# State-space stage: ScalarE prepares the FP4 rounding term, with a new table of steps

## Chip, cores and metric

The kernel runs on one core of one Trainium2 chip. The metric is the device time of one execution in microseconds, as the median of several runs.

## What is computed

The whole is two transformer-like layers in float32. The change touches the first layer only: a Mamba block and an FP4 feed-forward block side by side on the same normalized input, for 8 sequences of 512 rows, 256 columns each. Cut to what matters:

```python
xn = layernorm(x)                                  # (8, 512, 256)
x  = x + mamba(xn) + fp4_ffn(xn, w_gate, w_up, w_down)

def mamba(x):                                      # d_inner 512, d_state 16
    x_in, z = split(x @ W_in.T)
    u = silu(causal_conv4(x_in) + conv_b)
    d_raw, B, C = split(u @ W_xproj.T)             # 16, 16, 16
    delta = softplus(d_raw @ W_dt.T + b_dt)
    h[t] = exp(delta[t] * A) * h[t-1] + (delta[t] * u[t]) * B[t]
    y[t] = sum_n(h[t] * C[t]) + D * u[t]
    return (y * silu(z)) @ W_out.T

def fp4_quant_dequant(x):                          # blocks of 16 along the last axis
    scale = maximum(max(abs(xb)) / 6, 1e-12)
    idx = searchsorted([.25, .75, 1.25, 1.75, 2.5, 3.5, 5.], abs(xb / scale))
    return grid[idx] * sign(xb) * scale            # grid 0 .5 1 1.5 2 3 4 6

def fp4_ffn(x, ...):                               # hidden width 704
    h = silu(q(x) @ q(w_gate).T) * (q(x) @ q(w_up).T)
    return q(h) @ q(w_down).T
```

## The kernel before

The program has an FP4 preparation of the weights, then the stage `mamba_and_fp4_ffn`, then the second layer's attention and local-attention stages, which the change does not touch. The stage works through 8 batches (sequences). Each batch has 32 steps, here called units 0 to 31: unit u is one scan over 512 time steps for 128 channels and two states. Four channel groups of 8 units each make a batch.

In unit u the engines do this:

- ScalarE (ACT, L829 and L831) fills one of two halves of the PSUM tile `ps_dA` with exp(delta * A), called a fill below. It may start when unit u-2's product has left that half; for units 0 and 1 it waits for the whole batch before.
- GpSimd (POOL, L581) multiplies B with delta * u into a ring `hb` of eight buffers.
- VectorE (DVE) scans (L670), does the unit's extra work, and multiplies by C (L681).
- TensorE (PE, L1053) sums the product into `ps_y` with an identity matrix. At units 8, 16, 24 and at unit 0 of the next batch VectorE takes that sum and gates it (`gate_y`, L632), so these units wait until TensorE has summed the group before.

Everything else is woven in between as extra work behind a unit's own work: the projections and convolutions of the next batch, the four row tiles of the hidden layer of this batch, and the output sums of the batch before. Each engine works strictly in the order written. Which unit carries which piece is a table of numbers at the head of the function: `GATE`, `SILU`, `UP`, `XIN`, `CONV`, `Z`, `TURN_H` and so on, one entry for each tile or channel group. The buffers and semaphores decide whether a piece is ready.

The FP4 rounding is `fp4_part`, in three parts in three different units. Part 0 makes the blocks' scales. Part 1 (L125 to L127) multiplies by the inverse scale, takes the exponent bits of the result with a bitwise AND into the tile `work`, and turns them into 1.5 * 2^22 times the power of two, not less than 1.5 * 2^22. Part 2 (L129, L130) adds `work` and subtracts it, which rounds. It runs once a batch for the next batch's input `xn` (128 x 1024, units 11, 15, 18) and four times for the hidden tiles `h` (128 x 704, units 5 to 7, 22 to 24, 25 to 27, 29 to 31). All of these run on VectorE, with a semaphore between one and the next. The batches before the first and after the last carry parts of the work only: a prologue prepares batch 0 with no scans beside it, and the last batch prepares no other.

Of the kernel before, what the change touches and what calls it, by code (L numbers as in the profile page):

```python
# [215 lines left out]
def mamba_and_fp4_ffn(nc, io, W, x1_dram, bc_dram, NB):  # L216
# [22 lines left out]
    TURN_H, TAKE_H = [(9, 10), (28, 28), (30, 30), (1, 0)], [(11, 12), (28, 28), (31, 31), (0, 6)]  # L239

    FFN_SUM, TAKE_SUM = 28, 29
    X1, TAKE_X1 = [0, 1, 3, 5], [2, 6]

    Z, TAKE_Z, MOVE_Z = [13, 16, 26, 22], [15, 17, 27, 22], 17
# [7 lines left out]
    XD, TAKE_XD = 18, 19
    STORE = 14

    DT, ABS, LN = [19, 20, 24, 5], [20, 21, 24, 6], [24, 22, 24, 8]
    SOFT = [("abs", 0), ("relu", 0), ("exp", 0), ("abs", 1), ("relu", 1), ("exp", 1), ("ln", 1), ("abs", 2), ("relu", 2),
            ("exp", 2), ("ln", 0), ("ln", 2), ("abs", 3), ("relu", 3), ("exp", 3), ("ln", 3)]


    NORM, SCALE_X, DU, ADD = [3, 4, 5, 6], 20, [33, 6, 11, 23], [27, 29, 31, 16]  # L260

    SCALE_H = [9, 26, 29, 0]

    PAIRED = []

    with ExitStack() as ctx:
# [221 lines left out]
        def _(pool):  # L488
# [46 lines left out]
            def own(b, s, prev):  # L535
# [16 lines left out]
                if s - 3 in PAIRED:  # L552
                    r = s - 3
                    pool.wait_ge(weighed.s, weighed.at(b, r + 1))
                    pool.tensor_tensor(hb[:, r % RING, 0, :], hb[:, r % RING, 0, :], hb[:, r % RING, 1, :], ALU.add)\
                        .then_inc(paired.s, 1)
# [1916 lines left out]
```

## Time and profile before

| | us |
|---|---|
| median of 3 runs | 3510.61 (3509.2 to 3513.47) |
| the profiled execution: time | 3512.49 |
| its span, first to last instruction | 3510.6 |
| first scan starts | 140.52 |
| last gate of the stage starts | 1367.33 |
| from unit 0 to unit 0, batches 1 to 6 | 154.1 to 154.5 |

The span counts from the first to the last instruction of the core. Times in the timeline run from the span's start. Eight batches lie between the first scan and the last gate; the weights and the prologue are ahead of them, and the second layer behind them takes the rest. In the views PE is TensorE's matmuls, DVE is VectorE, ACT is ScalarE, POOL is GpSimd. A group's row gives busy time, mean duration in ns, and the idle time of its engine just ahead of it with what ended it.

### The profile page before, as it was taken

To read this page: it belongs to the slowest core of one execution; us is meant where nothing else is said; L and a number is where in the kernel's file an instruction comes from. 1 tells how busy PE (TensorE), PEld (TensorE's weight loads), DVE (VectorE), ACT (ScalarE), POOL (GpSimd) and SP (SyncE) were. 2 spreads that over 40 slices of the span, in tenths; PEclk is the share of its full clock that TensorE was granted. 3 is DMA by queue.
4 is the path that set the end of the run, shared out by engine and by line. 5 is a ranking of instruction groups with operands and counts; after the bars stand their busy time and mean duration, and the time that the engine had idled before them with its cause. 6 is when DMAs were issued, how large, how long until landed. Compare 5 with 4: busy or idle time off the path is not lost. (4 is left out here: it accounts for less than half of the span.)

```text
span 3510.6 us, 50669 instructions
## 1 busy us (share of the span) xinstructions
PE 3200.0 (91%) x16204; PEld 1867.5 (53%) x16204; DVE 2497.7 (71%) x3778; ACT 1771.1 (50%) x4156; POOL 1581.7 (45%) x974
## 2 busy tenths in 40 slices
PE   1799999989899986999999889999999999999997
PEld 1245454454445443566666546666666666666665
DVE  5499999999999995677776655555555555555563
ACT  1575867768685752556665433333333333333332
POOL 0456665666656562000000055555555555555552
PEclk9899999999999998999999989999999999999999
DMA  1466666766667582211000000000001100000000
GB/s 51 150 228 218 233 236 212 249 213 240 215 229 240 207 275 87 91 36 36 24 24 18 25 7 18 18 18 18 18 18 36 48 25 24 24 24 18 24 18 18
DMA packets 146655, 343.31 MB, mean 98 GB/s; under 512 B 14898, under 2 KB 78470, under 8 KB 146582
## 3 DMA queue, kind: packets, MB, share of 16 engines
q1 hardware_dynamic: 138134, 334.02, 28.1%
q10 hardware_dynamic: 8448, 8.39, 0.7%
q8 instruction: 37, 0.61, 0.1%
q14 instruction: 36, 0.29, 0.0%
HBM read 320.87 MB, written 21.50 MB: 98 GB/s over the span
## 5 line engine op out<-in xcount | busy, mean ns | idle before, releaser
L581 POOL TENSOR_TENSOR hb<-bcB,du 128x1024 f32<-128x1024 f32 x256 | 601.3, 2351 | 318.2 <-DVE hb L681 278.7
L670 DVE TENSOR_TENSOR_SCAN ps_dA<-ps_dA,hb 128x1024 f32<-128x1024 f32 x256 | 585.8, 2288 | 63.7 <-ACT ps_dA L831 63.4
L1053 PE MATMUL ps_y<-hb,ident 128*128 128x512 f32 x1024 | 496.5, 613 | 71.1 <-DVE hb L681 71.1
L1888 POOL TENSOR_TENSOR c_pr<-c_pr,c_inv 128x512 f32<-128x512 f32 (+1 forms) x256 | 233.4, 933 | 382.6 <-DVE c_inv L2010 382.6
L1053 PEld LDWEIGHTS ps_y<-hb,ident 128*128 128x128 f32 x1024 | 188.5, 193 | 310.7 <-issue 184.1
L1418 ACT ACTIVATE b_pr<-b_ps_s,b_negmax 128x256 f32<-128x256 f32 (+1 forms) x512 | 263.4, 526 | 163.8 <-DVE b_negmax L1332 161.4
L2127 ACT ACTIVATE c_pr<-c_ps_s,c_negmax 128x256 f32<-128x256 f32 (+1 forms) x512 | 223.3, 446 | 228.0 <-DVE c_negmax L1992 151.0
L831 ACT ACTIVATE ps_dA<-delta,a_neg 128x511 f32<-128x511 f32 x512 | 330.1, 676 | 1.1
L681 DVE TENSOR_TENSOR hb<-ps_dA,bcC 128x1024 f32<-128x1024 f32 x256 | 312.2, 1219 | 6.1 <-issue 0.3
L2371 PE MATMUL c_ps_s<-c_hT,c_w 128*128 128x512 f32 x576 | 260.9, 599 | 0.9 <-ACT c_hT L2170 0.9
L1865 POOL TENSOR_TENSOR c_q_cos<-c_q_cos,c_q_sin 128x1024 f32<-128x1024 f32 x64 | 150.8, 2357 | 232.1 <-DVE c_q_sin L1972 232.1
L1332 DVE TENSOR_REDUCE b_negmax<-b_ps_s 128x2 f32<-128x512 f32 (+1 forms) x320 | 204.6, 683 | 70.5 <-PE b_ps_s L1489 69.5
L1276 POOL TENSOR_TENSOR b_xb<-b_xb,b_o_bias 128x1024 f32<-128x1024 f32 x8 | 18.8, 2345 | 495.7 <-DMA b_xb<-x_scratch 495.7
L2214 PE MATMUL c_ps_s<-c_w_qkv,c_xT 128*128 128x512 f32 x512 | 237.6, 607 | 0.7 <-ACT c_xT L2100 0.7
L1503 PE MATMUL b_ps_t<-ident,b_pr 128*128 128x128 f32 x1280 | 189.0, 284 | 24.7 <-DVE b_pt L1354 12.8
L1871 POOL TENSOR_TENSOR c_rn<-c_ssc,c_mhalf 128x16 f32<-128x16 f32 x64 | 186.3, 2912 | 33.7 <-DVE c_ssc L1982 33.4
L2106 ACT ACTIVATE c_sq<-c_ps_s 128x512 f32<-128x512 f32 x128 | 69.5, 595 | 254.9 <-PE c_ps_s L2214 254.9
L1503 PEld LDWEIGHTS b_ps_t<-ident,b_pr 128*128 128x128 f32 x1280 | 136.0, 141 | 114.1 <-DVE b_pt L1354 55.9
L1489 PE MATMUL b_ps_s<-b_kf,b_qm 32*128 32x256 f32 (+1 forms) x1024 | 177.2, 459 | 0.9 <-ACT b_kf L1391 0.9
L2017 DVE COPY c_pt<-c_ps_t 128x512 f32<-128x512 f32 (+1 forms) x256 | 155.2, 616 | 24.5 <-PE c_ps_t L2264 23.9
L2295 PE MATMUL c_ps_o<-c_w,c_hid 128*128 128x256 f32 x768 | 172.4, 381 | 0.0
L2371 PEld LDWEIGHTS c_ps_s<-c_hT,c_w 128*128 128x128 f32 x576 | 105.4, 191 | 123.1 <-issue 121.1
(245 smaller groups left out, 6221.4 us busy)
## 6 DMA issues: line engine op xcount, KB each, us to landing
bcB<-bc_scratch SPq DMA_DIRECT2D x256, 512.0 KB, 4.4
bcC<-bc_scratch SPq DMA_DIRECT2D x256, 512.0 KB, 4.7
c_x<-stream_scratch SPq DMA_DIRECT2D x16, 512.0 KB, 5.3
c_xr<-stream_scratch SPq DMA_DIRECT2D x16, 512.0 KB, 4.2
xn<-in_x_dram SPq DMA_DIRECT2D x8, 512.0 KB, 5.4
xr<-in_x_dram SPq DMA_DIRECT2D x8, 512.0 KB, 5.3
x_scratch<-xr SPq DMA_DIRECT2D x8, 512.0 KB, 7.1
b_x<-x_scratch SPq DMA_DIRECT2D x8, 512.0 KB, 4.4
```

The source lines that it names most:

```text
L581: pool.tensor_tensor(hb[:, s % RING, :, :], bcB[:, s % ROWS, :, :], bc(du[:, c % 2, :].unsqueeze(1), [P, NG, T]), ALU.mult)\
L670: dve.tensor_tensor_scan(flat(h_all), flat(h_all), flat(tile), 0.0, ALU.mult, ALU.add)\
L681: dve.tensor_tensor(tile, h_all, bcC[:, s % ROWS, :, :], ALU.mult).then_inc(weighed.s, 1)
L831: last = act.activation(dA[:, s % 2, n, 1:], delta[:, c, 1:], ACT.Exp, scale=a_neg[:, c, g * NG + n:g * NG + n + 1])
L1053: last = pe.matmul(ps_y[:, :], W["ident"][:, :], hb[:, r % RING, i, :], start=False, stop=(g == GROUPS - 1 and i == terms - 1))
L1332: dve.tensor_reduce(negmax[:, u, 0:heads], ps_s[:, u % 4, :].rearrange("p (h n) -> p h n", h=heads), AX.X, ALU.max, negate=True).then_inc( ...
L1418: last = act.activation(pr[:, u % 8, cols], ps_s[:, u % 4, cols], ACT.Exp, bias=negmax[:, u, i:i + 1], accum_out=den[:, qt, h:h + 1])
L1503: last = pe.transpose(ps_t[:, u % 2, k * P:(k + 1) * P], pr[:, u % 8, k * P:(k + 1) * P], W["ident"][:, :])
L1888: pool.tensor_tensor(rows, rows, bc(inv[:, u, :].unsqueeze(2), [P, 2, w]), ALU.mult)\
L2127: last = act.activation(pr[:, u % 6, i * w:(i + 1) * w], ps_s[:, u % 4, i * w:(i + 1) * w], ACT.Exp, scale=-1.0 if s < AHEAD else 1.0, bia ...
L2214: last = pe.matmul(ps_s[:, pair(t) + a, :], xT[:, k, t * P:(t + 1) * P], w_qkv[:, k, a * INNER:(a + 1) * INNER], start=(k == 0), stop=(k = ...
L2371: last = pe.matmul(ag(j, a), w_1[:, k, at:at + P], hT[:, k, :], start=(k == 0), stop=(k == DC - 1))
```

## The change

Part 1 keeps the multiplication only, now by the negated inverse scale. ScalarE then makes |x| * (2^22 - 4) into `work` (`fp4_lift`, one ACTIVATE with Abs). Part 2 becomes two fused VectorE instructions: max(work, 1.5 * (2^22 - 4)) + x, and the same maximum minus the result. The two `tensor_scalar` instructions of part 1 are gone for these tiles; the weights' preparation is as before. Part 2 waits for the lift, and the lift waits for part 1 and for the last reader of `work`. ScalarE does the lift behind the fill that follows the unit of part 1 (`LIFT_X`, `LIFT_H`). The unused pairing of sums on POOL goes, and a semaphore is merged into another.

```diff
+LIFT = 2.0 ** 22 - 4.0
+CLAMP = 1.5 * LIFT
 def fp4_part(dve, st, rows, blk, work, p, n, part):
...
-        return st.done(dve.tensor_scalar(inv, inv, 1.0 - 2.0 ** -24, None, ALU.mult))
+        return st.done(dve.tensor_scalar(inv, inv, 2.0 ** -24 - 1.0, None, ALU.mult))
     if part == 1:
         dve.wait_ge(st.s, st.at(st.k))
-        st.link(dve.tensor_tensor(blocks, blocks, bc(inv.unsqueeze(2), [p, g, 16]), ALU.mult))
-        st.link(dve.tensor_scalar(w.bitcast(U32), rows.bitcast(U32), EXPONENT, None, ALU.bitwise_and))
-        return st.done(dve.tensor_scalar(w, w, 1.0, 1.5 * 2.0 ** 22, ALU.max, ALU.mult))
-    dve.wait_ge(st.s, st.at(st.k))
-    st.link(dve.tensor_tensor(rows, rows, w, ALU.add))
-    return dve.tensor_tensor(rows, rows, w, ALU.subtract)
+        return st.done(dve.tensor_tensor(blocks, blocks, bc(inv.unsqueeze(2), [p, g, 16]), ALU.mult))
+    st.link(dve.scalar_tensor_tensor(rows, w, CLAMP, rows, ALU.max, ALU.add))
+    return dve.scalar_tensor_tensor(rows, w, CLAMP, rows, ALU.max, ALU.subtract)
+
+def fp4_lift(act, rows, work, p, n):
+    return act.activation(work[0:p, 0:n], rows, ACT.Abs, scale=LIFT)
...
-    GATE, SILU, UP = [1, 19, 22, 25], [2, 21, 23, 25], [3, 21, 24, 25]
+    GATE, SILU, UP = [1, 18, 22, 25], [2, 20, 24, 26], [2, 21, 24, 25]
     HIDDEN = [5, 22, 25, 29]
+    LIFT_X, LIFT_H = XQ[1], [x + 1 for x in HIDDEN]
...
-    XIN, TAKE_XIN = [8, 9, 9, 14], [8, 11, 13, 15]
+    XIN, TAKE_XIN = [7, 8, 11, 12], [8, 10, 13, 14]
...
+                    if part == 2:
+                        dve.wait_ge(x_lifted.s, x_lifted.at(n, 1))
...
+                        if part == 2:
+                            dve.wait_ge(h_lifted.s, h_lifted.at(b, t + 1))
...
+                if s == LIFT_X:
+                    act.wait_ge(x_steps.s, x_steps.at(n, 2 * TT + 1 + FP4_OVER))
+                    if not isinstance(n, int) or n:
+                        act.wait_ge(hg_ready.s, hg_ready.at(n - 1, 1))
+                    fp4_lift(act, xn[:, :, :].rearrange("p t d -> p (t d)"), work, P, TT * D).then_inc(x_lifted.s, 1)
...
+            def lift_h(b, s, more):
+                for t in range(TT):
+                    if s == LIFT_H[t]:
+                        act.wait_ge(h_steps.s, h_steps.at(b, t * FP4_PARTS + FP4_OVER))
+                        if t == 1 and more:
+                            act.wait_ge(xg_ready.s, xg_ready.at(b + 1, 1))
+                        else:
+                            act.wait_ge(hg_ready.s, hg_ready.at(b, t))
+                        fp4_lift(act, h[:, HB[t], :], work, P, I).then_inc(h_lifted.s, 1)
...
+                        lift_h(b, s - 1, more)
                         ffn(b, s - 1)
```

The table moves some 25 pieces of work by one to four units on TensorE, ScalarE and GpSimd. On VectorE the units of the extra work stay as they were. In the loop over batches ScalarE has 27 table loads a batch before and 25 now.

ScalarE around units 25 to 28, before: the fill of unit 26 with its load, then the SiLU of the fourth hidden tile (`sg`, L804), then the fill of unit 27.

```order
L829 ACTIVATE ps_dA<-nought 128x2 [waits a_weighed]
L831 ACT_TABLE_LOAD
L831 ACTIVATE ps_dA<-delta,a_neg 128x511 x2
L802 REGISTER_ALU
L804 ACT_TABLE_LOAD [waits a_h]
L804 ACTIVATE sg<-ps_p 128x704 [waits a_gated]
L826 REGISTER_ALU
L829 ACTIVATE ps_dA<-nought 128x2 [waits a_weighed]
L831 ACT_TABLE_LOAD
L831 ACTIVATE ps_dA<-delta,a_neg 128x511 x2
```

And now: the fill of unit 27, the lift of the third hidden tile (L136), the SiLU of the fourth (L830), the gate z, and the fill of unit 28.

```order
L855 ACTIVATE ps_dA<-nought 128x2 [waits a_weighed]
L857 ACT_TABLE_LOAD
L857 ACTIVATE ps_dA<-delta,a_neg 128x511 x2
L814 REGISTER_ALU
L136 ACTIVATE work<-h 128x704 [waits a_hg,a_h_steps]
L828 REGISTER_ALU
L830 ACT_TABLE_LOAD [waits a_h]
L830 ACTIVATE sg<-ps_p 128x704 [waits a_gated]
L725 ACTIVATE z<-ps_t 128x512 [waits a_y,a_z_proj]
L852 REGISTER_ALU
L855 ACTIVATE ps_dA<-nought 128x2 [waits a_weighed]
L857 ACT_TABLE_LOAD
L857 ACTIVATE ps_dA<-delta,a_neg 128x511 x2
```

The fourth tile's SiLU stands one fill later than before, and behind a lift that waits for VectorE.

TensorE around units 25 and 26, before: `gate` and `up` of the fourth hidden tile (L993) between two sums.

```order
L1053 MATMUL ps_y<-hb,ident 128x512 [waits a_weighed]
L1053 MATMUL ps_y<-hb,ident 128x512
L993 MATMUL ps_p<-gateT,xqT 128x352 [waits a_h]
L993 MATMUL ps_p<-gateT,xqT 128x352 x3
L970 REGISTER_ALU
L993 MATMUL ps_p<-upT,xqT 128x352 [waits a_sg]
L993 MATMUL ps_p<-upT,xqT 128x352 x3
L1050 REGISTER_ALU
L1053 MATMUL ps_y<-hb,ident 128x512 [waits a_weighed]
L1053 MATMUL ps_y<-hb,ident 128x512
```

And now, with a projection for z (L891) ahead of them:

```order
L1076 MATMUL ps_y<-hb,ident 128x512 [waits a_weighed]
L1076 MATMUL ps_y<-hb,ident 128x512
L955 REGISTER_ALU
L891 MATMUL ps_t<-xnT,w_in 128x512 [waits a_soft]
L891 MATMUL ps_t<-xnT,w_in 128x512
L1020 MATMUL ps_p<-gateT,xqT 128x352 [waits a_h]
L1020 MATMUL ps_p<-gateT,xqT 128x352 x3
L997 REGISTER_ALU
L1020 MATMUL ps_p<-upT,xqT 128x352 [waits a_sg]
L1020 MATMUL ps_p<-upT,xqT 128x352 x3
L1074 REGISTER_ALU
L1076 MATMUL ps_y<-hb,ident 128x512 [waits a_weighed]
```

The `up` matmuls (the second pair with `upT`) wait for `sg`, and the next sum stands behind them as before.

TensorE around units 6 to 8, before: the sums of units 6 and 7, then the first projection of the next batch (L864) and its convolution (L898).

```order
L1053 MATMUL ps_y<-hb,ident 128x512 [waits a_weighed]
L1053 MATMUL ps_y<-hb,ident 128x512
L1050 REGISTER_ALU
L1053 MATMUL ps_y<-hb,ident 128x512 [waits a_weighed]
L1053 MATMUL ps_y<-hb,ident 128x512
L890 ISA
L864 MATMUL ps_p<-xnT,w_in 128x512 [waits a_xnT]
L864 MATMUL ps_p<-xnT,w_in 128x512
L896 REGISTER_ALU
L898 MATMUL ps_p<-xin,diag_c 128x512 [waits a_xin]
L898 MATMUL ps_p<-xin,diag_c 128x512 x3
```

And now: the first projection stands ahead of the sum of unit 7, the second right behind it, and the convolution comes after the next sum.

```order
L1076 MATMUL ps_y<-hb,ident 128x512 [waits a_weighed]
L1076 MATMUL ps_y<-hb,ident 128x512
L917 ISA
L891 MATMUL ps_p<-xnT,w_in 128x512 [waits a_xnT]
L891 MATMUL ps_p<-xnT,w_in 128x512
L1074 REGISTER_ALU
L1076 MATMUL ps_y<-hb,ident 128x512 [waits a_weighed]
L1076 MATMUL ps_y<-hb,ident 128x512
L891 MATMUL ps_p<-xnT,w_in 128x512 [waits a_xnT]
L891 MATMUL ps_p<-xnT,w_in 128x512
L1072 MATMUL ps_y<-u,diag_d 128x512 [waits a_y]
```

The convolution no longer follows its own projection directly.

## Rows read from the trace of the kernel before

**Rows 1.** Busy time by stretch: two parts of a batch, and one batch.

```profile
core 0: us, PE busy (x) PEld busy (x) DVE busy (x) ACT busy (x) POOL busy (x), PEclk, DMA share, GB/s
604.18:680.08 75.90, 73.53 (x218) 38.94 (x219) 71.17 (x61) 50.03 (x87) 53.59 (x30) 1.00 0.74 256
680.08:758.29 78.21, 68.72 (x195) 33.00 (x193) 75.10 (x65) 58.30 (x93) 44.33 (x23) 1.00 0.58 201
...
605.59:759.69 154.10, 142.24 (x414) 71.94 (x413) 146.26 (x126) 108.32 (x179) 97.90 (x53) 1.00 0.66 228
```

**Rows 2.** Waits of DVE, 160 to 1400 us: us in total, times, longest.

```profile
DVE y L632 <- PE ps_y L1053: 19.9, 11, 2.1
DVE h L648 <- PE ps_p L993: 13.5, 13, 1.8
DVE ps_dA L670 <- ACT ps_dA L831: 13.1, 13, 1.5
```

**Rows 3.** Groups of instructions on DVE by form, 0 to 1450 us.

```profile
L125 DVE TENSOR_TENSOR h<-h,blk_h 128x704 f32<-128x704 f32 x32 | 34.3, 1070 | 0.0
...
L632 DVE TENSOR_TENSOR y<-ps_y,z 128x512 f32<-128x512 f32 x32 | 22.0, 687 | 20.1 <-PE ps_y L1053 19.9
...
L126 DVE TENSOR_SCALAR work<-h 128x704 uint32<-128x704 uint32 x32 | 16.9, 527 | 1.1
...
L127 DVE TENSOR_SCALAR work<-work 128x1024 f32<-128x1024 f32 x8 | 5.6, 694 | 0.3
```

**Rows 4.** Timeline of DVE in that batch: start us, us, instruction.

```profile
605.59 2.30 DVE L670 TENSOR_TENSOR_SCAN ps_dA<-ps_dA,hb 128x1024 f32<-128x1024 f32 x1 [1.46 <-ACT ps_dA L831]
...
634.71 0.91 DVE L125 TENSOR_TENSOR h<-h,blk_h 128x704 f32<-128x704 f32 x1
635.66 0.53 DVE L126 TENSOR_SCALAR work<-h 128x704 uint32<-128x704 uint32 x1
...
636.66 1.22 DVE L681 TENSOR_TENSOR hb<-ps_dA,bcC 128x1024 f32<-128x1024 f32 x1
...
673.62 0.69 DVE L126 TENSOR_SCALAR work<-xn 128x1024 uint32<-128x1024 uint32 x1
...
674.96 1.22 DVE L681 TENSOR_TENSOR hb<-ps_dA,bcC 128x1024 f32<-128x1024 f32 x1
...
680.44 0.69 DVE L632 TENSOR_TENSOR y<-ps_y,z 128x512 f32<-128x512 f32 x1 [2.06 <-PE ps_y L1053]
...
726.79 2.29 DVE L670 TENSOR_TENSOR_SCAN ps_dA<-ps_dA,hb 128x1024 f32<-128x1024 f32 x1
...
737.46 2.29 DVE L670 TENSOR_TENSOR_SCAN ps_dA<-ps_dA,hb 128x1024 f32<-128x1024 f32 x1
...
741.01 2.29 DVE L670 TENSOR_TENSOR_SCAN ps_dA<-ps_dA,hb 128x1024 f32<-128x1024 f32 x1
```

**Rows 5.** Timeline of PE in that batch.

```profile
643.17 1.98 PE L1053 MATMUL ps_y<-hb,ident 128*128 128x512 f32 x4 [0.37 <-DVE hb L681]
...
678.37 1.88 PE L1053 MATMUL ps_y<-hb,ident 128*128 128x512 f32 x4
680.08 3.60 PE L898 MATMUL ps_p<-xin,diag_c 128*128 128x512 f32 x8
```

**Rows 6.** Timeline of ACT: one filling of ps_dA with a table load.

```profile
727.59 0.17 ACT L829 ACTIVATE ps_dA<-nought 128x2 f32<-128x2 f32 x1
727.77 1.28 ACT L831 ACT_TABLE_LOAD   x1
729.06 1.30 ACT L831 ACTIVATE ps_dA<-delta,a_neg 128x511 f32<-128x511 f32 x2
```

**Rows 7.** Groups of instructions on ACT by form, 450 to 1220 us.

```profile
L804 ACT ACTIVATE sg<-ps_p 128x704 f32<-128x704 f32 x20 | 15.1, 757 | 0.2
...
L721 ACT ACTIVATE z<-z 128x512 f32<-128x512 f32 x5 | 3.1, 613 | 0.0
```

**Rows 8.** Group on DVE in a later stage: a fused two-operation instruction.

```profile
L2076 DVE SCALAR_TENSOR_TENSOR c_hid<-c_ps_s,c_b_cols,c_gl 128x512 f32<-128x512 f32 x64 | 46.5, 744 | 106.1 <-ACT c_gl L2180 106.1
```

More of the change, by code:

```diff
@@ L230, in mamba_and_fp4_ffn @@
     RING, ROWS, LEAD = 8, 4, 3
-    GATE, SILU, UP = [1, 19, 22, 25], [2, 21, 23, 25], [3, 21, 24, 25]
+    GATE, SILU, UP = [1, 18, 22, 25], [2, 20, 24, 26], [2, 21, 24, 25]
     HIDDEN = [5, 22, 25, 29]
     HB = [0, 1, 0, 2]
[L239 to L244, printed above, removed]
+    XQ, TURN_XQ, TAKE_XQ = [11, 15, 18], 29, 30
+    LIFT_X, LIFT_H = XQ[1], [x + 1 for x in HIDDEN]
+    TURN_H, TAKE_H = [(9, 10), (26, 28), (30, 31), (0, 0)], [(11, 12), (27, 28), (31, 31), (1, 3)]
+    FFN_SUM, TAKE_SUM = 28, 30
+    X1, TAKE_X1 = [0, 1, 2, 3], [1, 5]
+    Z, TAKE_Z, MOVE_Z = [13, 16, 25, 22], [14, 18, 26, 22], 14
     ZPOS = [0, 1, 3, 2]
-    STATS, TURN_XN, TAKE_XN = 1, 4, 4
-    XQ, TURN_XQ, TAKE_XQ = [11, 15, 18], 29, 30
-    XIN, TAKE_XIN = [8, 9, 9, 14], [8, 11, 13, 15]
-    CONV, U = [8, 11, 15, 16], [10, 13, 16, 17]
+    STATS, TURN_XN, TAKE_XN = 1, 5, 6
+    XIN, TAKE_XIN = [7, 8, 11, 12], [8, 10, 13, 14]
+    CONV, U = [9, 10, 15, 16], [11, 11, 16, 17]
     MOVE_U = [27, 27]
[L252 to L264, printed above, removed]
+    XD, TAKE_XD = 17, 18
+    STORE = 10
+    DT, ABS, LN = [18, 20, 23, 5], [19, 21, 25, 7], [22, 22, 25, 7]
+    SOFT = [("abs", 0), ("relu", 0), ("exp", 0), ("abs", 1), ("relu", 1), ("exp", 1), ("ln", 0), ("ln", 1), ("abs", 2),
+            ("relu", 2), ("exp", 2), ("ln", 2), ("abs", 3), ("relu", 3), ("exp", 3), ("ln", 3)]
+    NORM, SCALE_X, DU, ADD = [3, 4, 5, 6], 24, [34, 3, 14, 21], [29, 30, 32, 15]
+    SCALE_H = [11, 27, 29, 1]
     with ExitStack() as ctx:
@@ L327, in mamba_and_fp4_ffn @@
         xr_in = S("a_xr_in", 16)
-        x_steps = S("a_x_steps", TT + 1 + FP4_STEPS)
-        h_steps = S("a_h_steps", TT * FP4_STEPS)
-        mv_ready = S("a_mv", TT)
+        x_steps = S("a_x_steps", 2 * TT + 1 + FP4_PARTS)
+        h_steps = S("a_h_steps", TT * FP4_PARTS)
         g_steps = S("a_g_steps", 2)
+        x_lifted = S("a_x_lifted", 1)
+        h_lifted = S("a_h_lifted", TT)
         xn_ready = S("a_xn", TT)
@@ L360, in mamba_and_fp4_ffn @@
         weighed = S("a_weighed", SCANS)
-        paired = S("a_paired", len(PAIRED))
         y0_done = S("a_y0", IC)
@@ L498, in prepare @@
                 if s == NORM[0]:
-                    pool.wait_ge(mv_ready.s, mv_ready.at(n, TT))
+                    pool.wait_ge(x_steps.s, x_steps.at(n, 2 * TT + 1))
                     pool.wait_ge(xn_ready.s, xn_ready.at(n, 0))
@@ L551, in own @@
                     scale_h(b - 1, TT - 1)
[L552 to L556, printed above, removed]
             def first(n):
@@ L614, in prepare @@
                     for t in range(TT):
-                        dve.bn_aggr(mv[:, t, :], stats[:, t, :]).then_inc(mv_ready.s, 1)
+                        xs.done(dve.bn_aggr(mv[:, t, :], stats[:, t, :]))
                 if s in XQ:
@@ L650, in ffn @@
                             dve.wait_ge(h_ready.s, h_ready.at(b, t + 1))
-                        last = fp4_part(dve, hs, rows, blk, work, P, I, s - HIDDEN[t])
-                        if s == HIDDEN[t] + 2:
+                        part = s - HIDDEN[t]
+                        if part == 2:
+                            dve.wait_ge(h_lifted.s, h_lifted.at(b, t + 1))
+                        last = fp4_part(dve, hs, rows, blk, work, P, I, part)
+                        if part == 2:
                             last.then_inc(hg_ready.s, 1)
@@ L1046, in body @@
                                 .then_inc(y0_done.s, 1)
-                        if r in PAIRED:
-                            pe.wait_ge(paired.s, paired.at(b, PAIRED.index(r) + 1))
-                        else:
-                            pe.wait_ge(weighed.s, weighed.at(b, r + 1))
-                        terms = 1 if r in PAIRED else NG
-                        for i in range(terms):
+                        pe.wait_ge(weighed.s, weighed.at(b, r + 1))
+                        for i in range(NG):
                             last = pe.matmul(ps_y[:, :], W["ident"][:, :], hb[:, r % RING, i, :],
-                                             start=False, stop=(g == GROUPS - 1 and i == terms - 1))
+                                             start=False, stop=(g == GROUPS - 1 and i == NG - 1))
                         last.then_inc(summed.s, 1)
```

1 line of the change is left out of this document (added).

## Prediction

> **What bounds the kernel now.** I read the busy times by stretch first, then the waits of DVE, then the timelines of one batch, the fourth of eight. In a batch of 154.10 us DVE is busy for 146.26, ACT for 108.32, POOL for 97.90 [rows 1]. DVE is the engine that sets the pace: its waits in the whole stage are few and short, 19.9 us for the sum `ps_y`, 13.5 for the hidden projections, 13.1 for ACT's fills [rows 2]. No row of the kind names POOL. So a microsecond taken off DVE can shorten the stage, as long as nobody else has to be waited for instead.
>
> The candidate for that is PE. It is busy for 142.24 us of the batch, and unevenly. From the sum of unit 31 to the sum of unit 15, which unit 16's gate waits for, it is busy for 73.53 of 75.90 us. In the other part, up to the next sum of unit 31, it is busy for 68.72 of 78.21 [rows 1]. In the first part PE, not DVE, is the bound: the gate at unit 16 waits 2.06 us for it [rows 4], and PE's own sum of unit 15 (678.37) runs straight into the next work at 680.08 with no idle ahead of it [rows 5]. The times are those of one profiled execution: 3512.49 us with a span of 3510.6; the median of the runs is 3510.61, 1.9 below its time. I make the sum against 3512.5 and take 1.9 off at the end.
>
> **The change, part by part.**
>
> *Removed from DVE.* Of each hidden tile two instructions of 527 ns go (L126 and L127 take the same), of each x tile two of 694 [rows 3]. In the timeline the first starts at 635.66 and the product by C at 636.66; with the small gap ahead and the overlap behind, a hidden tile's part 1 gets shorter by 2 x 0.527 + 2 x 0.03 = 1.12 us. The x tile's gets shorter by 2 x 0.694 + 0.04 = 1.43 (673.62 to 674.96 in the trace) [rows 4]. That is 4 x 1.12 = 4.5 us a batch for h and 1.4 for x, 5.9 together. Over the stage it is 32 x 1.12 + 7 x 1.43 = 45.8 us; the eighth x tile lies in the prologue, where DVE waits anyway.
>
> *The fused pair.* Part 2 keeps two instructions with the same two inputs in SBUF. The trace has no such instruction on SBUF alone. The nearest is a fused one with 512 columns and a PSUM input at 744 ns [rows 8], beside 687 for a plain product with 512 columns and a PSUM input [rows 3]. It clearly passes each column once. I take no extra cost, because the row's 57 ns come with a pointer operand that the new form lacks. The other end is 57 ns for each of 10 instructions a batch: 4.6 us in all. It can also be slightly below nothing if less is waited for; I keep 0 to +4.6.
>
> *Added to ACT.* The lift of a hidden tile: 613 ns for 512 columns from SBUF, 757 for 704 from PSUM [rows 7]. With the slope between them (0.75 ns a column) that is about 0.78 us for 704 columns, and about 1.0 for 1024. So 4 x 0.78 + 1.0 = 4.1 us a batch, against two table loads fewer, 2 x 1.28 = 2.6 [rows 6]. ACT rises from 108.3 to about 110 us of a batch: it hides, if the order lets it. A fill takes 1.35 us, 2.65 with its load (727.59 to 730.36) [rows 6]. Behind each unit I added up ACT's work of the new order and compared it with the time when the next fill is due. A lift waits for part 1, which ends 2.3 + 1.1 = 3.4 us after its scan starts [rows 3, 4], and DVE needs the lift only after the next scan; it is itself never late.
>
> *First part of the batch (to the sum of unit 15).* DVE saves 1.1 (unit 6) and 1.4 (unit 15) there, 2.5 us. But PE has to do the same 73.5 us of work. The new order puts the first two projections ahead of the convolution, so PE's short waits, like the 0.37 us at 643.17 [rows 5], can be filled; they were 75.90 - 73.53 = 2.4 us together. PE then arrives after 73.5 us and cannot arrive sooner. **Gain: 2.4 us.** The wait at unit 16 stays at about 2 us or grows, because 2.06 + 2.5 - 2.4 and the short waits of DVE ahead of it (0.7 us in units 4 and 5) land there.
>
> *Second part.* Three hidden tiles save 3 x 1.12 = 3.4 us. Between units 16 and 22 DVE saves nothing, and PE has the same work as before up to unit 22's projection, so that wait stays at 1.5 us. One new wait shows in the order. Count from the start of scan 26 (0): part 1 ends at 3.4, the lift at 4.2, the table load and SiLU of the fourth tile at 6.1, z at 6.6, the fill of unit 28 at 9.2. Scan 28 is due at 9.5: from scan 26 at 726.79 to scan 28 at 737.46 it was 10.67 [rows 4], less 1.12. PE's `up` matmuls wait for that SiLU and take about 2.4 us, to 8.6; a sum of 1.7 (678.37 to 680.08) [rows 5] ends at 10.3, the turned half of the second tile at 10.7. ACT copies it and two tiles of u by 12.4 and fills for unit 29 by 13.8. Scan 29 is due at 9.5 + 3.5 = 13.0 (737.46 to 741.01) [rows 4]. That costs 0.8 us. **Gain: 3.4 - 0.8 = 2.6 us.** The wait of 1.46 us at unit 0 [rows 4] stays: that fill waits for the whole batch before.
>
> *Ends.* The last batch has no x tile and little work on PE: 4.5 us gained. In the prologue PE's second projection no longer waits for ACT. Its convolutions there can end up to one projection earlier. A projection has as many matmuls as the sum that takes 1.7 us [rows 5], and all behind it starts earlier by that, less a little for the second copy: I take 1.5 us. ACT's lift falls into gaps between PE's deliveries. Bounds 0 and 3.
>
> **Sum.** 7 batches x (2.4 + 2.6) + 4.5 + 1.5 = 41.0 us. 3512.5 - 41.0 - 1.9 = 3469.6, say **3470**.
>
> The page "ScalarE: Activation LUTs" of the Trainium skill, under "Rules for kernel authors", speaks against the change: simple operations such as max, add and multiply are to stay on VectorE rather than move to ScalarE. Where ScalarE's time were the price, the rule would hold; the rows make its time hidden, and the sum above goes by them.
>
> **The rivals.**
>
> *A. PE gives the whole first part back.* PE's short waits don't close, because they belong to ACT's copies, and the gain of 2.4 becomes 0. For it: PE is busy for 97% there. Against: the new order separates each convolution from its own projection. 7 x 2.6 + 6 = 24 us gained: 3486.
>
> *B. Nothing stands in the way.* The new table also removes waits at units 16, 22 and 29: 45.8 us and 7 x 2.4 more from what DVE waited for there, less A's bound: 58 us, 3452. Against: 73.5 us of work on PE.
>
> *C. ACT becomes the bound.* Then each batch gains the DVE time less the lifts: 5.9 - 4.1 = 1.8 us, 7 x 1.8 + 1.4 = 14 us gained, 3497. For it: ACT's spare time is small from unit 17 to 28. Against: ACT is idle for 46 us a batch and loses two loads. This is how the page's rule would come out.
>
> *D. The lift holds ACT's queue: slower.* ACT works in order, so the SiLU and the fill behind a lift wait for DVE's part 1. The lift ends 4.2 us after the scan starts, where ACT would be done with the fill at 1.35; up to 2.8 us are lost to what is behind. For it: the fill of unit 28 has only 0.3 us to spare. From 5.0 / 4 = 1.25 us lost at each of the four hidden tiles on, the gain of a batch is gone. With 2 us at each it is 4 x 2 - 5 = 3 us a batch more, 7 x 3 - 6 = 15 us slower: 3526. Against: at the other three tiles the next fill has 1 us or more to spare.
>
> *E. The fused instruction isn't one pass a column.* At two passes each of ten instructions a batch would cost 0.7 to 1.1 us more, some 60 us: 3530. Against: 744 ns for 512 columns [rows 8].
>
> **Chances.** Forecast 0.68, A 0.13, B 0.05, C 0.06, D 0.06, E 0.02. The forecast's own spread is 3455 to 3480: the fused pair (+4.6), the prologue (1.5 either way), and 1 us a batch in the order (7 either way), with some of B's waits gone. The range for 8 in 10 takes in A: 3455 to 3486. A measurement of this kernel can tell about 0.2%, 7 us, from no change. Faster than that are the forecast, A, B and C: 0.91, as C is now and then nearer to nothing than I worked out. Within 0.2%: 0.04, from the milder ends of C and D. Slower: 0.05.
>
> **What would show it.** Right: L126 and L127 gone from the units of `h` and `xn`, about 5.9 us of DVE time less a batch; the two fused lines at about 890 ns for 704 columns; the lift at about 0.78 us; a batch of about 149.1 us; the wait at unit 16 still there with 2 to 3 us, named by `ps_y`; a new wait of under 1 us at unit 29, named by ACT's fill. Wrong in the first part: that stretch stays near 75.9 us (A) or falls below 73 (B). C or D would show as waits of DVE for `ps_dA` in units 17 to 28 that grow from 13 us to over 30. A fused line over 950 ns would be E.

## The result and the profile after

The changed kernel takes 3490.21 us (median of 4 runs, 3488.96 to 3491.78), the kernel before beside it 3510.81 (3509.2 to 3513.47): a ratio of 0.9941, 95% interval 0.9924 to 0.9958. It is faster by 20.6 us, half of the 41 us forecast, and lies 4 us above the range. The profiled execution took 3491.78 us with a span of 3489.9.

DVE's groups by form, 0 to 1450 us, answer to [rows 3], and ACT's, 450 to 1220 us, to [rows 7]:

```profile
L131 DVE SCALAR_TENSOR_TENSOR h<-work,h 128x704 f32<-128x704 f32 x32 | 33.0, 1032 | 0.0
L132 DVE SCALAR_TENSOR_TENSOR h<-work,h 128x704 f32<-128x704 f32 x32 | 28.5, 892 | 1.1
```

```profile
L136 ACT ACTIVATE work<-h 128x704 f32<-128x704 f32 x20 | 15.6, 780 | 9.7 <-DVE h L130 9.4
L136 ACT ACTIVATE work<-xn 128x1024 f32<-128x1024 f32 x5 | 5.3, 1058 | 0.0
```

The parts of the change came out as worked out. The fused pair is one pass a column, the lift costs ACT 0.78 and 1.06 us. DVE's busy time in the fourth batch fell from 146.26 us [rows 1] to 140.01 (-6.3, forecast -5.9):

```profile
core 0: us, PE busy (x) PEld busy (x) DVE busy (x) ACT busy (x) POOL busy (x), PEclk, DMA share, GB/s
594.72:663.30 68.58, 66.71 (x199) 35.75 (x199) 65.86 (x56) 45.67 (x81) 46.38 (x26) 1.00 0.74 264
663.30:748.13 84.83, 77.19 (x217) 38.03 (x216) 74.15 (x61) 63.58 (x102) 51.60 (x26) 0.96 0.60 203
594.72:748.13 153.41, 143.89 (x414) 73.78 (x414) 140.01 (x116) 109.24 (x182) 97.97 (x52) 0.98 0.66 230
```

The rows are the batch up to unit 16's scan, the rest of it, and the whole. The batch itself shrank by 0.7 us only, from 154.10 to 153.41, and PE's mean clock over it is 0.98 where it was 1.00. So 5.6 us of new idle time stand on DVE. Its waits, 160 to 1400 us, name the engine (they answer to [rows 2]):

```profile
DVE ps_dA L680 <- ACT ps_dA L857: 53.8, 26, 3.8
DVE y L639 <- PE ps_y L1076: 23.4, 21, 2.5
DVE h L655 <- PE ps_p L1020: 5.1, 7, 0.9
```

The wait for ACT's fills went from 13.1 to 53.8 us. It stands at four places. At **unit 0** it is 1.46 us in batch 1 and 3.36 to 3.58 in batches 2 to 6, where it was 1.46 [rows 4]; at **unit 4** it is 1.32 in batches 2, 4 and 6; at **unit 29** it is 2.4 to 2.5 in five batches and 3.6 to 3.9 in three; at **unit 22** it is 0.75 to 0.80 in seven, beside a wait for PE there that fell from 1.56 to 0.70. A batch, from one scan of unit 0 to the next, read off DVE's timeline:

| | first scan | batch 0 | batch 1 | batches 2 to 5 | batch 6 | last scan |
|---|---|---|---|---|---|---|
| before | 140.5 | 156.8 | 154.1 | 154.1 to 154.5 | 154.2 | 1360.1 |
| changed | 139.4 | 149.1 | 152.4 | 153.4 to 153.9 | 152.0 | 1338.9 |
| changed, ACT's loop moved by 32 instructions | 141.2 | 147.1 | 151.4 | 150.2 to 150.3 | 150.3 | 1322.5 |

The third line is the first experiment. The gain of the changed kernel lies mostly at the ends: 1.2 us in the prologue, 7.7 in batch 0, 6.2 in the last batch. Batches 1 to 5, each of which ends in a jump back of the loop, gain only 0.3 to 1.7 us each. ACT's timeline at the start of batch 4 shows why:

```profile
743.87 0.28 ACT L793 ACTIVATE hqT<-ps_t 128x128 f32<-128x128 f32 x1 [1.34 <-PE ps_t L1008]
744.05 0.26 ACT L794 ACTIVATE hqT<-ps_t 64x128 f32<-64x128 f32 x1
746.71 0.17 ACT L855 ACTIVATE ps_dA<-nought 128x2 f32<-128x2 f32 x1 [2.41 <-issue]
746.82 1.28 ACT L857 ACTIVATE ps_dA<-delta,a_neg 128x511 f32<-128x511 f32 x2
```

DVE's scan of unit 0 waits for that fill:

```profile
748.13 2.30 DVE L680 TENSOR_TENSOR_SCAN ps_dA<-ps_dA,hb 128x1024 f32<-128x1024 f32 x1 [3.50 <-ACT ps_dA L857]
```

ACT stands still for 2.41 us and waits for nothing that the profile shows ("issue"). It is the place where its loop jumps back. Section 3 of the profile's page has the queue that brings instructions: 36 packets before, 62 after.

```profile
q14 instruction: 36, 0.29, 0.0%
```

```profile
q14 instruction: 62, 0.50, 0.0%
```

### The profile page after: what moved, and what is told of

Its sections match the earlier page's. It is cut to its first block and busy times, and to the rows that moved or that the text cites. A ratio compares the mean times of both kernels' runs of the same rounds, so it can differ in the third digit from the quotient of the medians.

```text
span 3489.9 us, 50792 instructions
## 1 busy us (share of the span) xinstructions
PE 3199.1 (92%) x16204; PEld 1876.7 (54%) x16204; DVE 2445.8 (70%) x3698; ACT 1781.2 (51%) x4182; POOL 1583.0 (45%) x974
## 5 line engine op out<-in xcount | busy, mean ns | idle before, releaser
L1076 PE MATMUL ps_y<-hb,ident 128*128 128x512 f32 x1024 | 486.9, 604 | 32.0 <-DVE hb L691 31.9
```

Of the source, the lines that this page charges most:

```text
L1076: last = pe.matmul(ps_y[:, :], W["ident"][:, :], hb[:, r % RING, i, :], start=False, stop=(g == GROUPS - 1 and i == NG - 1))
```

## Experiments

The experiments carry the numbers in which they were made; those that answer the same question stand together.

**Theory F (fetch).** In the built program ACT's loop grew from 265 to 278 instructions and its start moved from instruction 306 to 315. The new rounding code did that: with the old code the new table gives 263 instructions from 304 on. If instructions come in blocks, the loop now lies across three blocks of instructions, and each jump back has to fetch the first again. **Theory U (the `up` matmuls):** at unit 29 the turned rows of tile 1 come late, because the `up` matmuls ahead of them wait 3.70 us for the SiLU. Rivals: the fills are late at unit 0 by the order of work itself; or the table, or the new code alone, does the harm.

**1. Move ACT's loop, nothing else.** ACT waits 64 times on a semaphore that is long satisfied (two waits to an instruction) ahead of everything. The changed kernel with these 64 waits is called the moved kernel below.

```
+            for _ in range(64):
+                act.wait_ge(s_w, 16 * 7)
```

> The changed kernel with 32 more instructions on ScalarE ahead of its loop (waits on a semaphore that is already there), nothing in the loop. Theory F (ScalarE's program in the loop now lies across one more block of instruction memory, so the jump back to its start has to fetch): the wait at unit 0 falls from about 3.5 us to 1.46 in batches 2 to 6, the instruction packets inside the loop go or become fewer, and the time falls by about 5 x 2.0 = 10 us, to about 3480. Rival R (the fill of unit 0 is late for a semaphore, such as the one from GpSimd for delta): nothing changes, about 3490; or, if the length of the loop alone decides, nothing changes either.

3477.27 us (3472.91 to 3479.11), ratio 0.9898 [0.9881, 0.9914]: 12.9 less than the changed kernel, for 32 useless instructions. The packets fell to 37 and the start of a batch looks like this:

```profile
738.11 0.26 ACT L796 ACTIVATE hqT<-ps_t 64x128 f32<-64x128 f32 x1
738.72 0.17 ACT L857 ACTIVATE ps_dA<-nought 128x2 f32<-128x2 f32 x1 [0.35 <-DVE hb L691]
```

DVE's wait at unit 0 is 1.46 us in all batches, and that of unit 4 is gone from the loop. What they exceeded that by in the changed kernel is 17.29 - 5 x 1.46 = 10.0 us at unit 0 and 3 x 1.32 = 4.0 at unit 4, 14.0 together, near the gain. F stands.

For this and all later comparisons: the kernel before took 3510.8 us beside the changed kernel and 3512.0 to 3512.8 beside the experiments, so against it the gain is 14.8 and not 12.9. The part behind the stage, which no edit touches, takes 2149.5 to 2154.3 us in the traces. So a few us between two medians say little, and where it matters the end of the stage in the trace is given too: the last scan starts at 1338.9 us in the changed kernel and at 1322.5 in this one.

**2. Take the SiLU of tile 4 a step earlier.** `SILU[3]` 26 to 25, `Z[2]` 25 to 26 with its copy at 27, tile 1 turned and taken at 28.

> The changed kernel with the fourth hidden tile's SiLU back in unit 25, its z projection in unit 26 and the second tile's turns in unit 28 as before the change. Theory U (PE's idle 3.7 us before the last up matmuls and the lower clock behind it make the fill of unit 29 late): the wait of up for sg falls below 2 us, the granted clock stays at 1.0 there, the wait at unit 29 falls from 2.5 to 3.6 us to under 1, the time falls by 7 x 2 = 14 us or more, to about 3475. Rival (the wait only moves, because ScalarE has as much to do in units 25 to 28): under 4 us gained, about 3487.

3515.4 us (3502.57 to 3524.21), ratio 1.0004 [0.9991, 1.0016]: 25 us slower than the changed kernel, a miss. The fetch is larger here: ACT's idle time put down to issue ahead of unit 0's fill is 5.2 to 5.5 us in batches 2, 4 and 6 and 2.2 to 2.3 in 3 and 5, there with a second one of 2.5 to 2.9 behind it.

**14. The same with ACT's loop moved** by the 64 waits.

> The table that takes the SiLU of the fourth tile one step earlier (3515.4 us, with its loop at 317 and two stalls at a jump), with the shift. Theory F: 37 packets, waits at unit 0 back from 10 and 3.3 us to 1.5. What is left is the table's own doing: it showed a wait of 3.96 us at unit 27 and none at 28 or 29, against 2.52 at unit 29, so about 1.4 us a batch more than the shifted changed kernel less what TensorE's early up matmuls save: batches of 151 us, 3483 us. Rival (the 10 us at unit 0 belong to the table): 3505 us or more.

3497.41 us (3494.5 to 3499.31), ratio 0.9959 [0.9945, 0.9974], a miss of 14 us again. The half of it about the fetch held in the main: 37 packets, no idle time of ACT put down to issue, and unit 0's wait from up to 10.3 us down to between 1.5 and 4.9 for the 1.5 expected. The other half, with what is left at unit 0, is the table's own. The SiLU now waits for PE (1.36 us), the softplus behind it delays the fill of unit 27 (DVE waits 3.95 us there in every batch, with the fetch and without), and PE, which waits 5.09 us for DVE, then needs 3.78 us for a sum that takes 1.88 elsewhere; the granted clock from 728 to 734 us is 0.50:

```profile
729.08 3.78 PE L1078 MATMUL ps_y<-hb,ident 128*128 128x512 f32 x4 [5.09 <-DVE hb L691]
732.65 1.06 PE L1010 MATMUL ps_t<-ident,h 128*128 128x128 f32 x4
```

**3, 4 and 8. The code and the table apart.** The new code with the old table (the lifts inserted one unit behind part 1), the old code with the new table, and the new code with the old table and the 64 waits.

> The new rounding code with the table of steps of the kernel before, lifts in the units of part 1 plus one. If the code alone is worth the DVE time it removes and the new table costs: about 3510.8 - 35 = 3475, below the changed kernel's 3490. If ScalarE can't carry the lifts in the old order (the new table is needed): 3490 to 3515. The loop on ScalarE is as long as in the changed kernel, so a wait of 3.5 us at unit 0 would stay with theory F.

> The old rounding code with the new table of steps. ScalarE's loop is 13 instructions shorter than in the changed kernel and starts 11 earlier, so with theory F no fetch and 1.46 us at unit 0. If the table in itself costs through PE's wait for the last SiLU: waits at unit 29 and 8 as in the changed kernel, 7 x 3 us slower than before, about 3525 to 3535. If the table is good in itself: 3505 or below.

> The new code under the old table of steps, with the shift: the code's part alone, free of the fetch. Without the shift it took 3494.5 us, with 61 instruction packets and waits at units 0 to 2 some 11 us over the undisturbed ones. Theory F: 37 packets, unit 0's wait 1.46 in every batch, batches 151.5 us apart, 3484 us. If the table then is worth what separates it from the shifted changed kernel (3477.3), it is 7 us. Rival (the waits at units 1 and 2 come of the lift under the old table): 3490 us or more.

3494.49 (ratio 0.9955 [0.9941, 0.9969]), 3500.47 (0.9967 [0.9955, 0.998]) and 3491.84 us (0.9933 [0.9915, 0.9952]). Beside the kernel before of their own runs (3512.7) the code without the fetch brings 21 us, the table alone 12, together 33; both together without the fetch bring 35. The two add up. The third is a miss by 8 us in its median (the lowest of its four runs was 3483.86), although its profile has what F expects: 37 packets, 1.46 us at unit 0, batches of 151.1 to 152.6 us. Under the old table the gate at unit 16 waits 3.5 us, where it waited 2.06 before: without the table, PE takes back more than half of what DVE saves in the first part. The fetch costs this table less: 2.7 us between the two medians, and 6.1 from first to last scan in the traces, where only batches 3, 4 and 6 show the stall by name.

**7. The reverse.** The kernel before gets 18 satisfied waits ahead of its loop and 26 inside, where ACT stood idle for 7.0 us; its loop then stands at 315 to 592, like the changed kernel's.

> The reverse test of theory F (instruction fetch at the jump back of ScalarE's loop): the kernel before, whose loop of 264 instructions begins at instruction 306, is given 18 satisfied waits (9 instructions) ahead of it and 26 (13 instructions) inside it, ahead of the wait for the turned rows, where ScalarE stood idle for 7.0 us; its loop then stands at 315 to 592, as the changed kernel's. No work is changed. Theory F: q14 carries about 62 instruction packets instead of 36, ScalarE shows an idle time of about 2.4 us put down to issue at the jump back, VectorE's wait at unit 0 goes from 1.46 to about 3.5 us in batches 2 to 6, and the time rises by 10 to 13 us, to about 3522 us. Rival (the late fills at unit 0 come of the change's own order of work on ScalarE): 36 packets, wait 1.46, 3511 us.

3515.68 us (3511.13 to 3520.84), ratio 1.0009 [0.9999, 1.0018]: the packets came (62), the 10 us did not. The trace tells why. In the kernel before, ACT waits for DVE's product at that place anyway; the stall runs beside that wait:

```profile
449.72 0.26 ACT L783 ACTIVATE hqT<-ps_t 64x128 f32<-64x128 f32 x1
452.33 0.18 ACT L834 ACTIVATE ps_dA<-nought 128x2 f32<-128x2 f32 x1 [2.35 <-DVE hb L681]
```

Undisturbed, that idle time is 1.47 to 2.96 us, different from batch to batch. In batch 2, shown here, DVE's wait at unit 0 rose from 1.46 to 2.34, by 0.88, as it would if the stall of 2.35 had 1.47 of cover. In batches 3, 4 and 6 DVE's product ends an idle time of ACT of 2.96 us, longer than the stall, and unit 0's wait is 1.46 as ever; in batch 5 the stall shows by name, and DVE's wait is 3.15 us:

```profile
917.97 0.17 ACT L834 ACTIVATE ps_dA<-nought 128x2 f32<-128x2 f32 x1 [2.28 <-issue]
```

In the changed kernel the cover is 0.35 us (the idle time there in the moved kernel), and 2.41 - 0.35 = 2.06 is what its wait grew by (3.50 - 1.46 = 2.04). So a fetch costs roughly what exceeds ACT's slack at the jump, and the change had taken that slack away as well.

**12 and 13. The same padding, by 4 and by 8 instructions.**

> The changed kernel with 8 satisfied waits (4 instructions) ahead of ScalarE's loop instead of 64 (32 instructions): its loop stands at 319 to 596, where it still covers three blocks of 256 instructions if theory F reads the fetches rightly. Theory F (the position decides, not that waits were added): 62 instruction packets, waits of 3.4 us at unit 0 in batches 2 to 6, 3490 us, as the changed kernel. Rival (any padding ahead of the loop helps, or shift of other timing): 37 packets or 3477 us.

> The changed kernel with 16 satisfied waits (8 instructions) ahead of ScalarE's loop: its loop stands at 323 to 600. The second stall of the run at 319 lies between the two exponentials of the first fill (instructions 322 and 323), that of the run at 317 ahead of the first exponential of the second fill (323 as well). Theory F with a block's edge at 323: this loop begins on the edge and covers two blocks; 37 packets, no idle put down to issue at the jump, unit 0's wait 1.46 us, 3477 us, though the loop is moved by only 4 instructions against the run that took 3513. Rival (the stalls have to do with the amount of padding or with other code): between 3490 and 3513 us, 60 packets.

3513.31 us (3511.3 to 3517.32) and 3474.61 (3472.18 to 3475.05), ratios 1.0005 [0.9995, 1.0014] and 0.9892 [0.9876, 0.9909]: four more instructions are worth 38.7 us. Against the changed kernel the second is 15.6 us less, with the first scan at 139.4 us as there; the 32 instructions of experiment 1 had it at 141.2. The first was expected at 3490: the packets were right and the time was not, since at 319 there are two stalls at a jump, the second between the two exponentials of the first fill:

```profile
437.55 0.17 ACT L857 ACTIVATE ps_dA<-nought 128x2 f32<-128x2 f32 x1 [2.28 <-issue]
437.66 0.67 ACT L859 ACTIVATE ps_dA<-delta,a_neg 128x511 f32<-128x511 f32 x1
442.21 0.69 ACT L859 ACTIVATE ps_dA<-delta,a_neg 128x511 f32<-128x511 f32 x1 [3.88 <-issue]
```

The two exponentials are instructions 322 and 323. That puts a block's edge at instruction 323 of the built program, and the run that starts at 323 agrees. With edges every 256 instructions from there, all kernels of this study fall into place (the seven not listed start at 347 or 349, lie in two blocks and have 37 or 38 packets):

| ACT's loop, instructions | kernel | blocks | q14 packets | DVE's wait at unit 0, batches 2 to 6 | us |
|---|---|---|---|---|---|
| 306 to 570 | before | 2 | 36 | 1.46 | 3510.8 |
| 304 to 566 | old code, new table | 2 | 37 | 1.46 | 3500.5 |
| 315 to 592 | changed | 3 | 62 | 3.36 to 3.58 | 3490.2 |
| 315 to 592 | before, at this place | 3 | 62 | 1.46 to 3.15 | 3515.7 |
| 317 to 596 | new code, old table | 3 | 61 | 1.84 to 3.35 | 3494.5 |
| 317 to 596 | changed, SiLU earlier | 3 | 61 | 3.30 to 10.34 | 3515.4 |
| 319 to 596 | changed, + 4 | 3 | 61 | 5.67 to 7.43 | 3513.3 |
| 323 to 600 | changed, + 8 | 2 | 38 | 1.46 | 3474.6 |
| 347 to 624 | changed, + 32 | 2 | 37 | 1.46 | 3477.3 |

The page "Runtime: NRT & Kernel Launch" of the Trainium skill, under "Instruction fetch mechanics", has the rule: most engines hold two blocks of 256 instructions, filled in sequence, and a taken branch to a block outside of them has to fetch it first. The packets in the table agree with it: 61 or 62 where the loop lies across three blocks, 36 to 38 where it lies across two. The price of a stall comes from the rows.

**5. Let TensorE work while it waits.** `UP[3]` goes from 25 to 26, in the moved kernel: PE then does the sum and turns tile 1 ahead of the `up` matmuls.

```
-    GATE, SILU, UP = [1, 18, 22, 25], [2, 20, 24, 26], [2, 21, 24, 25]
+    GATE, SILU, UP = [1, 18, 22, 25], [2, 20, 24, 26], [2, 21, 24, 26]
```

> The changed kernel, with the 64 satisfied waits ahead of ScalarE's batch loop (as in the first shifted run: 3477.3 us, batches 150.2 us apart) and the up matmuls of the fourth hidden tile one step later (26 in place of 25), so that TensorE does the sum of the group before and turns tile 1's first half while it waits for the SiLU, and the up matmuls come behind both. Theory T (unit 29's wait of 2.52 us is the turned rows of tile 1, late because they stand behind up matmuls that wait 3.70 us for the SiLU and then run at a granted clock of 0.72 in 4.08 us): the turn starts by 714 instead of 719 us, the rows are taken behind the fill, VectorE's wait at unit 29 falls from 2.5 to about 0.5 us, batches 148.2 us apart, 3463 us. Rival (unit 29's fill is late for another reason, the two copies of u or the buffer of sums): the wait stays 2.5, 3477 us.

3463.86 us (3460.26 to 3472.45), ratio 0.9856 [0.984, 0.9873], the lowest median of the study. The wait at unit 29 is gone altogether; U stands. The 3463 expected were met, but not by the 2 us a batch that they were worked out from. The profiled execution was the slowest of the four, and its batches are 150.2 us as before the edit: the second part of a batch is 1.4 us shorter (81.6 to 80.2), the first 1.4 us longer (68.6 to 70.0), with DVE's wait at unit 8 up from 1.98 to 2.44 and a new one of 0.78 us for POOL at unit 4. Which of that the three faster runs lack can't be read. The last scan starts at 1318.2 us, 4.3 earlier than in the moved kernel, where the medians differ by 13.4.

**6, 9 and 10. What TensorE's clock costs.** In the moved kernel, PE's rows at that place are

```profile
707.23 2.53 PE L1022 MATMUL ps_p<-gateT,xqT 128*128 128x352 f32 x8
713.46 4.08 PE L1022 MATMUL ps_p<-upT,xqT 128*128 128x352 f32 x8 [3.70 <-ACT sg L832]
```

The `gate` matmuls take 2.53 us and the same amount of `up` work, behind 3.70 us of waiting, 4.08; the granted clock from 712 to 718 us is 0.72. In the changed kernel it was 5.06 us at a clock of 0.50, TensorE's lower level (1.2 GHz):

```profile
718.28 5.06 PE L1020 MATMUL ps_p<-upT,xqT 128*128 128x352 f32 x8 [3.70 <-ACT sg L830]
```

```profile
718.00:724.00 6.00, 5.71 (x10) 3.17 (x11) 5.85 (x5) 3.37 (x6) 4.25 (x4) 0.50 0.61 223
```

Matmuls that add zeros to the running sum are put into the wait:

```
+                    if t == 3:
+                        for _ in range(22):
+                            pe.matmul(ps_y[:, 0:160], W["ident"][:, :], zeros[:, :], start=False, stop=False)
                     pe.wait_ge(sg_ready.s, sg_ready.at(b, t + 1))
```

> The changed kernel, shifted in the same way, with 22 matmuls of 160 columns of zeros into the running sum (they add nothing) in TensorE's wait of 3.70 us for the SiLU of the fourth hidden tile: no work is left out, and nothing waits for them. Theory C (TensorE's own idleness brings the granted clock down, and that makes the up matmuls long): clock 1.00 instead of 0.72 in that stretch, the up matmuls 2.5 us instead of 4.1, tile 1's rows turned 1.5 us earlier, VectorE's wait at unit 29 2.5 to about 1.0 us, about 10 us less over the kernel: 3467 us. Rival (the clock falls there for another reason, or its fall is no price): the up matmuls stay 4.1 us long or the wait 2.5 us, 3477 us or more.

> As the run with 22 matmuls of zeros, with 12. There they took 6.14 us (44 passes of 0.14 us), 2.3 us longer than the wait they filled, so that the up matmuls began that much late and gave back the 1.55 us that the clock of 1.00 saved them. Twelve take 3.35 us of the wait of 3.70. Theory C (idleness costs clock, and the clock costs time): the up matmuls take 2.5 us from the SiLU's end, tile 1's rows are turned 1.5 us earlier than in the shifted run without zeros, VectorE's wait at unit 29 falls from 2.5 to about 1.0 us, and the time from 3477 to about 3467 us. Rival (a bound elsewhere holds batches at 150.2 us): the wait falls and others grow, 3477 us.

With 22: 3476.19 us (3475.49 to 3479.24), ratio 0.9897 [0.988, 0.9913], no gain and a miss of 9 us. With 12: 3468.74 (3466.55 to 3473.55), ratio 0.9879 [0.986, 0.9898], 8.5 us less than without (last scan at 1315.9 us, 6.6 earlier). Rows of the first and the second:

```profile
710.39 6.14 PE L1003 MATMUL ps_y<-zeros,ident 128*128 128x160 f32 x44
716.37 2.53 PE L1027 MATMUL ps_p<-upT,xqT 128*128 128x352 f32 x8
```

```profile
706.84 3.42 PE L1003 MATMUL ps_y<-zeros,ident 128*128 128x160 f32 x24
710.70 2.63 PE L1027 MATMUL ps_p<-upT,xqT 128*128 128x352 f32 x8 [0.44 <-ACT sg L834]
```

Both keep the clock at 1.00 and the `up` matmuls at 2.5 to 2.6 us. Twenty-two were too many: SiLU was done at 714.2, and the matmuls began at 716.4. I had counted a matmul of zeros once, and the rows show each f32 matmul twice (x44 for 22). With 12 the wait at unit 29 fell from 2.53 us (the row below, from the moved kernel) to 0.81. So at that place of each batch the lower clock cost 1.5 us, and useless work in the wait bought it back.

```profile
722.93 2.30 DVE L680 TENSOR_TENSOR_SCAN ps_dA<-ps_dA,hb 128x1024 f32<-128x1024 f32 x1 [2.53 <-ACT ps_dA L859]
```

The same was tried at the batch's last sum, in the kernel of experiment 5, where PE waits 2.33 us and the sum took 3.60 us:

```profile
735.80 3.60 PE L1078 MATMUL ps_y<-hb,ident 128*128 128x512 f32 x4 [2.33 <-DVE hb L691]
```

> The shifted kernel with the up matmuls at 26 (3463.9 us), and 7 matmuls of zeros (14 passes of 0.14 us, 1.96 us) into the running sum in TensorE's wait of 2.33 us for the last product of a batch. There the clock then fell to 0.74 and the sum of the last group took 3.60 us instead of 1.88. Theory C: clock 1.00, the sum 1.9 us, the last hidden tile turned 1.7 us earlier, the gate's wait for the running sum at unit 8 down from 2.4 to about 1.0 us and the wait for POOL at unit 4 gone: 2 us a batch, about 3450 us, or, where the unprofiled runs already lack the drop, 3458 us. Rival: batches stay 150.2 us apart, 3464 us.

3466.05 us (3464.56 to 3467.46), ratio 0.9869 [0.9853, 0.9886]. The sum takes 1.88 us again, but the median is that of experiment 5 within its spread, where 3450 or 3458 was expected: a miss. Most of the time was not on the path. DVE's wait at unit 8 stayed between 1.94 and 2.45; the one for POOL at unit 4 went, with at most 0.41 us for ACT in its place in the loop, and the batches of the traces are 148.8 to 149.6 us for 150.2, where 2 us each were expected. That trace's last scan is 5.1 us earlier; the medians don't show it.

**11. Relax the fill of unit 0,** in the kernel of experiment 10. It waits for the product of unit 30, whose buffer it takes, not 31.

```
+                        elif s == 0 and (not isinstance(b, int) or b):
+                            act.wait_ge(weighed.s, weighed.at(b, 0) - 1)
```

> As the run before it, and ScalarE's first fill of a batch waits for the product of unit 30 (whose buffer it takes) instead of that of unit 31. That fill is what VectorE waits 1.46 us for at unit 0 in all kernels without a fetch. If nothing takes its place: up to 1.4 us a batch, 8 to 10 us less, about 3442 us. Rival (GpSimd's product for unit 0 or TensorE's first part is late next, as TensorE holds 73 us of work there): 0 to 4 us less.

3465.99 us (3464.51 to 3467.1), ratio 0.9869 [0.9852, 0.9886]: nothing gained on experiment 10. The rival held. The wait went in batches 1 and 5, stayed at 1.1 to 1.4 us in the others, and where it shrank, waits at units 4 (0.45 to 0.78 us) and 8 (2.43 to 2.45, for PE) took its place. In the moved kernel PE is busy for all of the first part:

```profile
589.90:658.50 68.60, 68.60 (x210) 37.37 (x209) 65.86 (x56) 45.68 (x81) 47.52 (x27) 1.00 0.80 272
```

## Why the prediction was half right

- **DVE's saving: right.** -6.3 us of busy time a batch against -5.9. The fused L131 averages 1032 ns where the plain addition took 977, L132 892 for 892: 32 x 0.055 = 1.8 us over the stage, inside the 0 to +4.6 of the sum. Rival E is refuted, though the sign given for it, "a fused line over 950 ns", showed: L131 is over 950, and so was the plain addition that it replaced.

```profile
L129 DVE TENSOR_TENSOR h<-h,work 128x704 f32<-128x704 f32 x32 | 31.3, 977 | 0.0
L130 DVE TENSOR_TENSOR h<-h,work 128x704 f32<-128x704 f32 x32 | 28.5, 892 | 1.1
```

- **The lift hides: right.** 0.78 and 1.06 us, never waited for by DVE inside the batches. ACT was busy for 109.24 of 153.41 us, so C did not decide. Nor did the rule of the Trainium skill ("ScalarE: Activation LUTs", "Rules for kernel authors") that keeps simple operations such as max, add and multiply on VectorE.
- **First part: right in kind, gain larger.** From unit 0's scan to unit 16's gate it was 74.85 us, and is 71.85 where no fetch disturbs it: 3.0 us for the 2.4 of the sum. PE is the bound, as worked out: in the moved kernel it is busy without a gap from the sum of unit 31 to the end of that of unit 15, and the same 218 matmuls take 72.9 us, a little less than the floor of 73.5 (row below). The sentence that the wait at unit 16 "stays at about 2 us or grows" was wrong: it is 0.92 us, and a wait of 1.95 stands at unit 8 now.

```profile
588.50:661.39 72.89, 72.89 (x218) 39.27 (x219) 68.19 (x57) 49.87 (x89) 51.27 (x29) 1.00 0.79 271
```

- **"The wait of 1.46 us at unit 0 [rows 4] stays: that fill waits for the whole batch before": the step that failed.** In batches 2 to 6 it was 3.36 to 3.58 us. The step asked what the fill waits for and not whether ACT could issue it. The lift's instructions in ACT's loop were costed by their duration and not by their place in the program. The fetch costs 12.9 us by experiment 1 and 15.6 by experiment 13, two thirds or more of the shortfall of 20.2 us to 3470.
- **"That costs 0.8 us" at unit 29: mis-sized.** It was 2.52 us in most batches, with the fetch and without, and 3.5 to 3.9 in some (in batches 3 and 5 only with the fetch). I took 2.4 us for the `up` matmuls at any clock; they took 4.1 to 5.1 after the wait of 3.70 us, which I had not written down as a wait of PE at all. With the clock kept, the wait was 0.81, the figure of the sum. 1.7 x 7 = 12 us.
- **The ends were larger than the sum had them:** batch 0 gained 7.7 for 5.0, the last 6.2 for 4.5 (the prologue 1.2 for 1.5). With the first part's 0.6 us in each of the six other batches this gave back about 8 of the 12. That is luck: nothing in the sum foresaw it.
- **D, the lift holding ACT's queue,** is what happened at unit 29 in part: the lift (0.77 us) stands ahead of the SiLU that PE waits for. Where it stands was not tested by itself. The sign for C or D, waits for `ps_dA` "in units 17 to 28 that grow from 13 us to over 30", did not show: of the 53.8 us only 5.3 stand there, at unit 22. It was a bad sign all the same. The 13 us it starts from stood at unit 0, and the harm done here stood at units 0, 4 and 29, outside the units that it watches.

## What to carry to other kernels

An edit that adds instructions to a rolled loop, or ahead of one, moves it over the blocks in which instructions come. Look for idle time put down to "issue" at the jump back and for more packets on the instruction queue, and move the loop's start past the edge with padding before judging the edit. Here one loop was worth 3474.6, 3490.2 or 3513.3 us by eight instructions. And when a wait of TensorE is added, cost the matmuls behind it at the lower clock as the worse end; give it real work to do in the wait, or, failing that, useless work that ends before the wait does.

## What was not expected of the hardware

- A jump back out of the held blocks stops ScalarE for 2.2 to 2.5 us (5.2 to 5.5 in three batches of experiment 2; why is open). A block's edge a few instructions behind the target adds 3.2 to 4.0 us in experiment 12 and 2.8 to 3.4 in experiment 3. A stall costs nothing as far as ScalarE waits there anyway.
- TensorE's granted clock fell at waits of 3.70 us (the means of 6 us are 0.50 from 718 to 724 us in the changed kernel and 0.72 from 712 to 718 in the moved one) and of 2.33 us (0.74 from 736 to 742 in experiment 5), and not behind one of 2.56 us in the same batch of experiment 5, where it stayed 1.00. What tells these apart is open.
- VectorE's instruction on 44 columns at L125 took 0.19 us at unit 29 in the moved kernel and 0.85 us in experiment 5, with GpSimd's products beside it (722.51 to 724.85 us); this and L127 took back 1.2 of the 2.5 us gained at unit 29. That GpSimd is the cause was not tested.
